# Cross attention's scores as three fp32r products, with queries and keys split into high and low parts batch by batch

## What is computed

```python
q_hk  = (layernorm(x) @ Wq.T).reshape(B, 32, 16, 128)
q_big = apply_rope(einsum('bshk,hkq->bshq', q_hk, w_kc_q), ...)
kv_r  = apply_rope(kv_c, ...)                         # [64, 257, 128]
q_r   = einsum('bshq,hqr->bhsr', q_big, W_qr)
k_r   = einsum('bld,hdr->bhlr', kv_r, W_kr)
scores = einsum('bhsr,bhlr->bhsl', q_r, k_r)
attn  = softmax(scores, axis=-1)
ctx_c = einsum('bhsl,bld->bhsd', attn, kv_r)
ctx   = einsum('bhsd,hkd->bhsk', ctx_c, w_kc_kv)      # then @ Wo.T
```

## Time and profile before

| | |
|---|---|
| Median of three runs | 1765.01 us (1761.34 to 1765.61) |
| The profiled execution: time, span | 1764.15 us, 1762.3 us |
| PE busy | 1547.7 us, 88% of the span |
| DVE busy | 1127.6 us, 64% |
| ACT busy | 810.1 us, 46% |
| POOL busy | 542.6 us, 31% |
| Mean granted TensorE clock | 0.943 of 2.4 GHz |
| First and last score product (L958) start | 471.9 and 958.2 us |

### The profile page before, as it was taken

The page is one execution under the profiler, slowest core; times in us unless marked ns, Lnnn a source line. Parts: engine busy times, 40 slices in busy tenths (PEclk is TensorE's granted clock), DMA queues, the critical chain, the costliest instruction groups (busy, mean ns, idle before and its releaser), DMA issues. The chain is left out here.

```text
span 1762.3 us, 26302 instructions
## 1 busy us (share of the span) xinstructions
PE 1547.7 (88%) x8136; PEld 1171.3 (66%) x8136; DVE 1127.6 (64%) x1818; ACT 810.1 (46%) x1723; POOL 542.6 (31%) x594
## 2 busy tenths in 40 slices
PE   5899999999559999999999399999758679898996
PEld 4577777777347777777777277787423258686775
DVE  6888887777257788877777224544356625464646
ACT  4565656565335555555554223433201244555553
POOL 5233443230144545455553121110041030403102
PEclk9899999999789999999999679999889879999998
DMA  4143233333384444454442130000143100000000
GB/s 159 42 123 97 88 108 109 108 100 110 103 277 110 120 110 119 114 119 113 116 113 60 54 130 0 0 0 0 72 191 140 51 0 1 25 1 24 0 25 24
DMA packets 137878, 143.46 MB, mean 81 GB/s; under 512 B 83168, under 2 KB 102752, under 8 KB 134112
## 3 DMA queue, kind: packets, MB, share of 16 engines
q1 hardware_dynamic: 136096, 133.60, 25.9%
q10 hardware_dynamic: 1728, 9.20, 1.6%
HBM read 113.27 MB, written 29.49 MB: 81 GB/s over the span
## 5 line engine op out<-in xcount | busy, mean ns | idle before, releaser
L901 ACT ACTIVATE c_e_t_high<-c_et_ps 128x512 fp32r<-128x512 f32 x128 | 76.7, 599 | 226.3 <-PE c_et_ps L966 226.3
L77 DVE TENSOR_TENSOR b_rot_parts_low<-b_rot,b_rot_parts_high 128x1536 fp32r<-128x1536 f32 x64 | 136.3, 2130 | 22.3 <-ACT b_rot_parts_high L526 22.3
L794 POOL TENSOR_TENSOR c_mixed_low<-c_whole,c_mixed_high 128x512 fp32r<-128x512 f32 x64 | 95.3, 1490 | 176.0 <-ACT c_mixed_high L913 176.0
L958 PE MATMUL c_sc_ps<-c_kv_t,c_q 128*128 128x257 f32 x512 | 136.3, 390 | 13.7 <-DMA c_q<-carried_queries 13.7
L1500 PE MATMUL f_ps<-f_right,f_left 128*128 128x512 f32 x256 | 115.9, 615 | 27.9 <-DMA f_right<-ent_out 20.6
L817 DVE TENSOR_REDUCE c_peak<-c_sc_ps 128x2 f32<-128x514 f32 x128 | 88.6, 692 | 54.5 <-PE c_sc_ps L958 53.8
L70 PE MATMUL e_mm_ps<-folded_high,e_h_t_high 128*128 128x512 f32 x256 | 108.7, 425 | 15.8 <-DVE e_h_t_low L77 15.7
L958 PEld LDWEIGHTS c_sc_ps<-c_kv_t,c_q 128*128 128x128 f32 x512 | 99.4, 195 | 32.9 <-DMA c_q<-carried_queries 14.5
L264 POOL TENSOR_TENSOR b_turned_raw<-b_turn_part 128x384 f32<-128x384 f32 x32 | 68.9, 2155 | 164.9 <-DVE b_key_parts_low L77 163.6
L309 DVE TENSOR_TENSOR b_rot<-b_w_qr,b_angle 128x1536 f32<-128x1536 f32 x64 | 118.9, 1858 | 0.2
L893 ACT ACTIVATE c_e<-c_sc_ps,c_peak 128x257 f32<-128x257 f32 x256 | 118.8, 475 | 0.0
(11 more groups left out here) (214 smaller groups left out, 4026.2 us busy)
## 6 DMA issues: line engine op xcount, KB each, us to landing
c_q<-carried_queries SPq DMA_DIRECT2D x64, 256.0 KB, 3.6
c_ends_spread<-end_weights SPq DMA_DIRECT2D x64, 256.0 KB, 4.3
carried_queries<-x SPq DMA_DIRECT2D x7, 2048.0 KB, 11.2
b_early<-early SPq DMA_DIRECT2D x15, 640.0 KB, 3.9
c_raw<-cache_t SPq DMA_DIRECT2D x64, 128.5 KB, 3.9
c_swapped<-cache_t SPq DMA_DIRECT2D x128, 64.2 KB, 3.8
f_left<-ent_in SPq DMA_DIRECT2D x8, 1024.0 KB, 5.1
f_right<-ent_out SPq DMA_DIRECT2D x8, 1024.0 KB, 7.8
```

Source lines behind the costliest of these rows:

```text
L77: return nc.vector.tensor_tensor(low, value, high.bitcast(F32), ALU.subtract)
L794: nc.gpsimd.tensor_tensor(mixed[1][:, w, :, u], whole[:, u % 2].rearrange("p (h s) -> p h s", h=H), mixed[0][:, w, :, u].bitcast(F32), ALU ...
L958: last = nc.tensor.matmul(sc_ps[:, 2 * half + c, 0:L], q[:, u, at], kv_t[:, u], start=True, stop=True)
```

## The change

Each batch's queries (128 x 512) and rotated context (`keys`, 128 x 257 with one zero column added, 258) get a high and a low part, and a score product becomes three fp32r products of 258 columns. ACT rounds both (`round_scoring`, for batch b+1 in the even step of batch b, and once before the walk), DVE takes the keys' low part (`split_keys`), POOL the queries' low part (`split_query`, between `keep_ends` and `rotate`). The parts have two places each. Raw queries have two places and not four, and SP's load of the queries of batch b waits until the queries of batch b-2 have been split (`q_split`), where it waited for the scores of batch b-4. `rotate` no longer waits for `scored`.

```diff
--- before.py
+++ after.py
@@ -683,9 +683,12 @@
         table, raw, swapped = crossing.table, crossing.raw, crossing.swapped
         table_loaded, raw_loaded = crossing.table_loaded, crossing.raw_loaded
         part = sb("c_part", [P, 2, L])
-        kv_t = sb("c_kv_t", [P, BT, L])
+        kv_t = sb("c_kv_t", [P, BT, L + 1])
         kv = pair("c_kv", [P, BT, 2, P])
-        q = sb("c_q", [P, BT, H * S])
+        LE = L + 1
+        q = sb("c_q", [P, 2, H * S])
+        q_parts = pair("c_q_parts", [P, 2, H * S])
+        keys = pair("c_keys", [P, 2, LE])
         peak = sb("c_peak", [P, 2, 2])
         total = sb("c_total", [P, 2, 2])
         inverse = sb("c_inverse", [P, 2, 2])
@@ -704,7 +707,9 @@
         out_ps = ctx.enter_context(nc.psum_tensor("c_out_ps", [P, D], F32))
         kv_ps = ctx.enter_context(nc.psum_tensor("c_kv_ps", [P, D], F32))
         x_loaded = sem("c_x_loaded")
-        q_loaded = [sem(f"c_q_loaded{u}") for u in range(BT)]
+        q_loaded = [sem(f"c_q_loaded{v}") for v in range(2)]
+        keys_rounded, keys_split, q_rounded, q_split, padded = (
+            sem(f"c_{n}") for n in ("keys_rounded", "keys_split", "q_rounded", "q_split", "padded"))
         rotated_, kv_turned, kv_rounded, kv_split, pool_chained = (
             sem(f"c_{n}") for n in ("rotated", "kv_turned", "kv_rounded", "kv_split", "pool_chained"))
         scored, peaked, exped, normed = sem("c_scored"), sem("c_peaked"), sem("c_exped"), sem("c_normed")
@@ -755,8 +760,8 @@
                     if isinstance(b, int) and b == BT:
                         sp.wait_ge(crossing.last_out[1], 16)
                         sp.wait_ge(crossing.last_out[2], 16)
-                    wait(sp, scored, 2 * (b - BT) + 2)
-                    sp.dma_start(q[:, u], q_in[bass.ds(b, 1)].rearrange("b d x -> d (b x)")).then_inc(q_loaded[u], 16)
+                    wait(sp, q_split, b - 1)
+                    sp.dma_start(q[:, u % 2], q_in[bass.ds(b, 1)].rearrange("b d x -> d (b x)")).then_inc(q_loaded[u % 2], 16)
                     if known(i, 1):
                         spread_ends(i - 1, u)
                 sp.dma_start(x1[:, bass.ds(i, 1)].rearrange("p t d -> p (t d)"),
@@ -776,11 +781,14 @@
                 nc.gpsimd.tensor_tensor(part[:, 0], raw[:, u], table[:, 0], ALU.mult).then_inc(pool_chained, 1)
                 nc.gpsimd.tensor_tensor(part[:, 1], swapped[:, u], table[:, 1], ALU.mult).then_inc(pool_chained, 1)
                 pool.wait_ge(pool_chained, 2 * b + 2)
-                wait(pool, scored, 2 * (b - BT) + 2)
                 wait(pool, kv_turned, b - BT + 1)
                 wait(pool, mix_taken, b - BT + 1)
-                nc.gpsimd.tensor_tensor(kv_t[:, u], part[:, 0], part[:, 1], ALU.add).then_inc(rotated_, 1)
+                nc.gpsimd.tensor_tensor(kv_t[:, u, 0:L], part[:, 0], part[:, 1], ALU.add).then_inc(rotated_, 1)
                 pool.wait_ge(rotated_, b + 1)
+
+            def split_query(b, v):
+                pool.wait_ge(q_rounded, b + 1)
+                nc.gpsimd.tensor_tensor(q_parts[1][:, v], q[:, v], q_parts[0][:, v].bitcast(F32), ALU.subtract).then_inc(q_split, 1)
 
             def keep_ends(n, i, u, half):
                 pool.wait_ge(normed, n + 1)
@@ -794,7 +802,9 @@
                 nc.gpsimd.tensor_tensor(mixed[1][:, w, :, u], whole[:, u % 2].rearrange("p (h s) -> p h s", h=H),
                                         mixed[0][:, w, :, u].bitcast(F32), ALU.subtract).then_inc(mix_split, 1)
 
+            nc.gpsimd.memset(kv_t[:, :, L:], 0.0).then_inc(padded, 1)
             rotate(0, 0, 0)
+            split_query(0, 0)
             rotate(1, 1, 0)
 
             def tile(i, w):
@@ -802,6 +812,8 @@
                     n, u, half = STEPS * i + j, j // 2, j % 2
                     b = BT * i + u
                     keep_ends(n, i, u, half)
+                    if half == 0 and not (isinstance(b, int) and b + 1 >= B):
+                        split_query(b + 1, (u + 1) % 2)
                     if half == 0 and not (isinstance(b, int) and b + 2 >= B):
                         rotate(b + 2, (u + 2) % BT, i + (u + 2) // BT)
                     if half == 1 and (u or known(i, 1)):
@@ -827,6 +839,10 @@
                 dve.wait_ge(et_rounded, n + 1)
                 at = slice(2 * P * half, 2 * P * (half + 1))
                 low_part(nc, e_t[1][:, u % 2, :, at], et_ps[:].rearrange("p (k x) -> p k x", k=2), e_t[0][:, u % 2, :, at]).then_inc(et_split, 1)
+
+            def split_keys(b, u):
+                dve.wait_ge(keys_rounded, b + 1)
+                low_part(nc, keys[1][:, u % 2], kv_t[:, u], keys[0][:, u % 2]).then_inc(keys_split, 1)
 
             def split_kv(b, u):
                 dve.wait_ge(kv_rounded, b + 1)
@@ -868,6 +884,8 @@
                     split_turned(n, u, half)
                     if half == 0:
                         split_kv(b, u)
+                        if not (isinstance(b, int) and b == B - 1):
+                            split_keys(b + 1, (u + 1) % BT)
                     if j == 2 and known(i, 2):
                         add_out(i - 2)
                     if more:
@@ -875,6 +893,7 @@
                     if j == 4 and known(i, 2):
                         keep_moments(i - 2)
 
+            split_keys(0, 0)
             find_peak(0, 0)
             normalise(0, 0)
             in_tiles(dve, tile)
@@ -901,6 +920,16 @@
                 nc.scalar.activation(e_t[0][:, u % 2, :, 2 * P * half:2 * P * (half + 1)], et_ps[:].rearrange("p (k x) -> p k x", k=2),
                                      ACT.Copy).then_inc(et_rounded, 1)
 
+            def round_scoring(b, t, u):
+
+                act.wait_ge(rotated_, b + 1)
+                if isinstance(b, int) and b == 0:
+                    act.wait_ge(padded, 1)
+                wait(act, scored, 2 * (b - 2) + 2)
+                nc.scalar.activation(keys[0][:, u % 2], kv_t[:, u], ACT.Copy).then_inc(keys_rounded, 1)
+                act.wait_ge(q_loaded[u % 2], 32 * t + 16 * (u // 2) + 16)
+                nc.scalar.activation(q_parts[0][:, u % 2], q[:, u % 2], ACT.Copy).then_inc(q_rounded, 1)
+
             def round_kv(b, u):
                 act.wait_ge(kv_turned, b + 1)
                 wait(act, mix_done, b - BT + 1)
@@ -931,6 +960,8 @@
                         exponential(n + 1, 1 - half)
                     if half == 0:
                         round_kv(b, u)
+                        if not (isinstance(b, int) and b == B - 1):
+                            round_scoring(b + 1, i + (u + 1) // BT, (u + 1) % BT)
                     if half == 1 and (u or known(i, 1)):
                         round_mixed(b - 1, (u - 1) % BT, i if u else i - 1, w if u else 1 - w)
                     if j == 3 and known(i, 2):
@@ -940,6 +971,7 @@
 
             for ab in range(2):
                 act.wait_ge(crossing.w_vo_out[ab], 32 * H // 2)
+            round_scoring(0, 0, 0)
             exponential(0, 0)
             in_tiles(act, tile)
             round_mixed(B - 1, BT - 1, TILES - 1, 1)
@@ -950,12 +982,13 @@
         def _(pe):
             def score(n, b, t, u, half):
                 if half == 0:
-                    pe.wait_ge(q_loaded[u], 16 * (t + 1))
-                    pe.wait_ge(rotated_, b + 1)
+                    pe.wait_ge(q_split, b + 1)
+                    pe.wait_ge(keys_split, b + 1)
                 wait(pe, exped, n - 1)
                 for c in range(2):
                     at = slice((2 * half + c) * P, (2 * half + c + 1) * P)
-                    last = nc.tensor.matmul(sc_ps[:, 2 * half + c, 0:L], q[:, u, at], kv_t[:, u], start=True, stop=True)
+                    last = multiply_parts(nc, sc_ps[:, 2 * half + c, 0:LE], [a[:, u % 2, at] for a in q_parts],
+                                          [a[:, u % 2] for a in keys], True, True)
                 last.then_inc(scored, 1)
 
             def turn_weights(n, half):
```

## The result

The changed kernel takes **2248.5 us** (median of four runs, 2245.9 to 2253.0) where the kernel before takes 1765.3 beside it: a ratio of 1.2746, with a 95% interval from 1.2714 to 1.2777. The forecast was 2222 in a range of 2119 to 2305. The profiled execution took 2251.07 us (span 2249.2), 487 more than the 1764.15 of before; its mean granted clock is 0.864, where it was 0.943.

What follows compares the result with a forecast made beforehand. TensorE was taken to bound cross attention; the change would close a loop through SP's queue, 14.7 us a batch for 7.63. 1764 + 424 (loop) + 2 (start) + 5 (end) + 27 (clock) = 2222 us, range 2119 to 2305.

Steps and rivals of the forecast that it cites:

- Store to spread: SP's queue, from storing the end weights to spreading them: 1.93 us with a query load 0.89 us ahead.
- POOL's split: POOL's split_query of 512 columns in the even step: 1.47 us by L794, against 1.26 alone.
- the first scores: Start of cross attention: PE's first scores wait for a query copy and split, +2 us.
- the last four batches: End of cross attention: no query load ahead of the spread; three batches take 9.0 us, not 7.4: +5 us.
- The clock: PE in cross attention: 5.6 us of idle a batch lowers the clock, 0.45 us in every turn, +27 us.
- The case that the clock holds: Rival: PE is at 2.4 GHz whenever it turns weights, so the 0.45 us goes: 2195 us; 15%.
- The shorter loop alone: Rival: a quicker spread leaves only the loop from POOL's split to scores, 9.0 us a batch: 1853 us; 7%.
- The queue is slower: Rival: SP's wait for the store is 3.7 us longer throughout, 60 x 3.7 more: 2444 us; 5%.
- Faster: Rival: cheaper score products on PE take 18 us off, 1746 us, if the split query is there in time; 3%.
- These products save nothing here: PE's score products: its 4.1 us of work end before 9.7 us, so cheaper products save nothing, dearer ones cost nothing.
- the long loop: Loop through SP's queue, DVE, PE, ACT and POOL's query split: 14.7 us a batch for 7.63, +424 us; 84%.
- By throughput all fit: Added work fits in 7.4 us a batch: ACT 4.0 + 1.1, DVE 5.9 + 0.4, POOL 3.7 + 1.5.

Runs made afterwards that it cites:

- the run with early parts: Changed kernel with query and key parts made half a batch earlier and the end weights' spread issued ahead of SP's query load: 1934.6 us, ratio 1.0972.
- the last kernel: Changed kernel with spread before query load, parts made early, both low parts on POOL, query split between keep_ends and split_mixed: 1753.4 us, ratio 0.9947.
- the run with the spread first: Changed kernel with SP issuing spread_ends ahead of the wait for q_split and the query load: 1929.7 us, a batch of 10.2 us.

## Why the prediction was right

**What bounds, and by how much.** The step that carried the forecast was that `spread_ends(c)` is issued behind a load that waits for `split_query(c+2)`, which closes a loop through DVE. The 60 waits of SP, the 61 of `add_end`, and the last four quick batches are what it named; freeing the spread alone, by either of two edits, took away two thirds of the loss. Its terms against the mean of 45 turns, worked out from the trace as start-to-start or end-to-start distances:

| one turn, us | forecast | measured |
|---|---|---|
| SP wakes | 0.10 | 0.16 |
| query load to store | 0.89 | 0.64 |
| store to spread | 1.93 | 2.48 |
| spread to L858 | 4.23 | 4.17 |
| L858 to the end of L836 | 2.59 | 2.51 |
| to PE's turns and ACT's L920, clock included | 1.21 | 1.23 |
| L920 to the end of the query copy | 2.66 | 2.61 |
| POOL wakes | 0.10 | 0.08 |
| POOL's query split | 1.47 | 1.68 |
| sum | 15.15 (14.7 and 0.45, as rounded there) | 15.57 |

**What was off.** Two terms of the turn were too small, and they make nearly all of the 26 us between 2222 and 2248.5. *Store to spread* was taken with the query load 0.89 us ahead; here it is 0.64 ahead, and the store takes longer to come back behind it: together 3.12 for 2.82. *POOL's split* was taken at the mean of L794; in this place it starts in the same moment as `normalise` (both at 899.83) and takes 1.82 us there, 1.68 on the mean of these turns. The turn was 0.42 short, 60 x 0.42 = 25 us. The rest is small and partly cancels: batches stood 7.56 us apart before, from `add_end` to `add_end`, not 7.63 (4 us more); the first scores come 3.2 us later (475.05 for 471.89), not 2 (1 more); the last four batches and what follows together cost nothing, where I had 5 (5 less); and the 59 distances average 15.62, a little over the 45 turns of the table (3 more). That makes 28 of the 29 us by which the profiled execution exceeds the sum.

**The clock.** I took the half clock from the turns after 5.51 us of idle, 0.45 a turn. After 5.62 us of idle the four turns took 1.12 us, and filling the idle time gave back 0.44 to 0.48. The case that the clock holds (15%) did not come true in any long turn: from the end of `normalise` to ACT's start each took 1.21 or 1.29 us.

**The rivals.** *The shorter loop alone* (9.0 us a turn, 1853) was the right mechanism for what lies beneath, but its price was too low: alone it gives 1930. My 9.0 took full clock for granted; with the clock held it measures 9.37. *The queue is slower* was right in sign: 0.3 us a turn, not 3.7. *Faster* (18 us by PE's time) does not come even with the parts left out, which gives 7 to 8 us. The score products cost 0.12 us as taken (901.93 to 902.05), so weight loads set no pace. The rule of the Trainium skill (FP8 and Floating Point Precision, TensorE Precision Notes), that true FP32 makes four passes, gives the estimate that three of them are 3/4 of a plain f32 product; they measure 0.36 of 0.43, five sixths, and by that rule alone the forecast would have had the wrong sign. "These products save nothing here" held in the long loop: PE is done with its scores at 905.94, 3 us before DVE gets the spread (908.99).

**By throughput all fit** was true only as a sum. That DVE and POOL cannot run some operations beside each other was in none of my terms, though 1.47 against 1.26 us for the same POOL operation was its trace in the kernel before: 62 of the 64 overlap a `normalise` and take 1.50 us on the mean, the two that do not take 1.27. In the changed kernel it costs 0.4 us a turn (1.68 for 1.26); with the parts made half a batch early it was, together with the order on DVE, what kept the kernel at 1935 us.

## What to carry to other kernels

When a wait is moved on a queue, work out at which step its semaphore is reached, and who waits for what is queued behind it; a short transfer behind a load with a late wait can close a loop round four engines. Then look beneath: the next loop (10.2 us), the clock that falls in it, and the order of single DVE and POOL operations each had to be mended before the cheaper product was worth its 0.5%. A new long POOL operation belongs where DVE has no operation with two SBUF inputs that anybody waits for.

## What the hardware showed that I had not expected

DVE and POOL hold each other up for whole instructions, in both directions. In the run with early parts DVE's 128x258 difference took 1.29 us for 0.42, and `normalise` 1.56 for 0.69, each ending 0.3 to 0.6 us behind the POOL operation that was under way; in the changed kernel POOL's split, starting together with `normalise`, took 1.82 us for 1.26. In one turn of four of that kernel DVE has `add_out` (one input in PSUM) ahead of `normalise`, so POOL starts first: it takes 1.28 us, and `normalise` stands instead, 0.99 us for 0.69.

```profile
619.58 1.28 POOL L791 TENSOR_TENSOR c_q_parts_low<-c_q,c_q_parts_high 128x512 fp32r<-128x512 f32 x1 [2.62 <-ACT c_q_parts_high L931]
...
620.42 0.99 DVE L836 TENSOR_TENSOR c_e<-c_e,c_inverse 128x512 f32<-128x512 f32 x1
```

DVE operations with one input in PSUM (`split_turned` and `split_kv`) were not touched: in the last kernel, with POOL busy 317 of 400 us (560 to 960 us), they take 686 and 425 ns, where they took 688 and 425 before. The Trainium skill (SBUF — State Buffer, SBUF: two separate sides) states this: the pair of ports that both engines share is a lock, held for the whole instruction, and a DVE operation with two SBUF inputs takes it against a GpSimd one that reads SBUF. The runs agree.

The store of the end weights came back in 2.5 us with a query load of 256 KB 0.64 us ahead on the same queue, in 1.44 with nothing ahead (1.79 on the mean in the run with the spread first).

PE's clock fell in every turn with 5.6 us of idle in it, though PE was busy 59% of that stretch, and in part of the batches of the shorter loop, with only 2.2 us of idle a batch ahead of the scores and 78% busy (mean granted clock 0.89). Dense products in the gap brought it to 1.00.
